# State copies moved from VectorE to ScalarE in a two-direction Mamba scan, with the chunk loops written out

## What is computed

```python
xz = x @ win.T;  u, z = split(xz)                 # 1024 channels each
u = silu(causal_conv4(u) + bconv)
dbc = u @ wx.T;  dt, B, C = dbc[:, :32], dbc[:, 32:48], dbc[:, 48:64]
delta = softplus(dt @ wdt.T + bdt);  A = -exp(Alog)
h_t = exp(delta_t * A) * h_(t-1) + (delta_t * u_t) * B_t     # 16 states n per channel
y_t = sum over n of h_t * C_t, + u * Dp, * silu(z);   y @ wout.T
```

## Time and profile before

| | |
|---|---|
| median of 3 runs | 7603.56 us (7603.14 to 7606.13) |
| profiled execution, its own time | 7600.66 us |
| its span in the profile | 7598.7 us |
| busy share of the span | PE 90%, DVE 92%, ACT 80%, POOL 92% |
| granted TensorE clock, mean | 0.973 |

### The profile page before, as it was taken

One profiled execution on the slowest core, in us unless ns is written; L12 is line 12 of the kernel. 1 busy time (PEld: TensorE's weight loads), 2 busy tenths in 40 slices (PEclk: granted clock), 3 DMA queues, 4 the chain that ended last, 5 costly groups with the idle time before them and its releaser, 6 DMA issues. The chain is left out here.

```text
span 7598.7 us, 137446 instructions
## 1 busy us (share of the span) xinstructions
PE 6830.6 (90%) x32682; PEld 4035.6 (53%) x32682; DVE 6955.4 (92%) x10093; ACT 6069.6 (80%) x11545; POOL 6968.9 (92%) x3774
## 2 busy tenths in 40 slices
PE   6899999899898989999898999999898999999889
PEld 3455555555555555555555555555555555555455
DVE  2799999999999999999999999999999999999766
ACT  1788888888788888888788888888788888888645
POOL 0899999999999999999999999999999999999678
PEclk8999999999999999999999999999999999999999
DMA  8444445444444454444445544444355444444555
GB/s 258 145 137 134 128 139 149 128 120 144 132 134 126 141 150 124 123 143 138 122 129 145 149 113 136 139 137 134 117 150 149 107 141 135 138 130 131 152 193 172
DMA packets 605609, 1066.02 MB, mean 140 GB/s; under 512 B 113584, under 2 KB 221872, under 8 KB 596336
## 3 DMA queue, kind: packets, MB, share of 16 engines
q1 hardware_dynamic: 602704, 1055.84, 46.9%
q10 hardware_dynamic: 2080, 1.05, 0.0%
HBM read 926.61 MB, written 130.05 MB: 139 GB/s over the span
## 5 line engine op out<-in xcount | busy, mean ns | idle before, releaser
L692 POOL TENSOR_TENSOR dBu<-Bb,du 128x1024 f32<-128x1024 f32 x2048 | 4787.8, 2365 | 74.9 <-DVE hV L1153 44.2
L1153 DVE TENSOR_TENSOR_SCAN scans<-scans,state,dBu 128x512 f32<-128x512 f32 x2304 | 2902.8, 1280 | 393.6 <-ACT scans L806 363.1
L806 ACT ACTIVATE scans<-delta,A 128x512 f32<-128x512 f32 x4096 | 2745.7, 691 | 557.4 <-DVE hC L1169 480.9
L1016 PE MATMUL yT<-ident,hC 128*128 128x128 f32 x9216 | 1407.4, 282 | 344.1 <-DVE hC L1169 340.8
L1169 DVE TENSOR_TENSOR hC<-scans,Cb 128x512 f32<-128x512 f32 x2304 | 1556.8, 680 | 12.2 <-PE yT L1016 12.2
L1016 PEld LDWEIGHTS yT<-ident,hC 128*128 128x128 f32 x9216 | 1058.6, 143 | 774.8 <-DVE hC L1169 536.4
L701 POOL TENSOR_TENSOR hR<-hR,Cb 128x512 f32<-128x512 f32 x1024 | 1290.0, 1270 | 190.2 <-DVE state L1183 183.7
L1153 DVE TENSOR_TENSOR_SCAN hR<-scans,state,dBu 128x512 f32<-128x512 f32 x1024 | 1293.4, 1263 | 0.5
L1009 PE MATMUL bg<-u,comb 128*128 128x512 f32 x2112 | 989.1, 594 | 0.9 <-DVE u L1125 0.9
L1153 DVE TENSOR_TENSOR_SCAN hV<-scans,state,dBu 128x512 f32<-128x512 f32 x768 | 968.6, 1261 | 13.1 <-ACT scans L806 12.8
L948 PE MATMUL bg<-hT,win_u 128*128 128x512 f32 x2112 | 966.5, 598 | 0.9 <-ACT hT L728 0.9
(11 more groups left out here) (163 smaller groups left out, 7586.9 us busy)
## 6 DMA issues: line engine op xcount, KB each, us to landing
comb<-pre_scratch SPq DMA_DIRECT2D x1040, 256.0 KB, 4.6
Bb<-bc_scratch SPq DMA_DIRECT2D x264, 512.0 KB, 8.6
Cb<-bc_scratch SPq DMA_DIRECT2D x264, 512.0 KB, 7.9
win_u<-in_win SPq DMA_DIRECT2D x264, 256.0 KB, 4.9
pre_scratch<-pre SPq DMA_DIRECT2D x264, 256.0 KB, 3.7
comb<-comb_scratch SPq DMA_DIRECT2D x66, 1024.0 KB, 8.0
win_z<-in_win SPq DMA_DIRECT2D x257, 256.0 KB, 2.7
part_scratch<-pre SPq DMA_DIRECT2D x132, 256.0 KB, 2.0
```

Source lines behind the costliest of these rows:

```text
L692: pool.tensor_tensor(dBu[:, q % AHEAD], Bb[:, 2 * q:2 * q + 2, :], du[:, j % 2, :].unsqueeze(1).broadcast_to([P, 2, T]), ALU.mult).then_in ...
L806: act.activation(place(n)[:], delta[:, j % 2, :], ACT.Exp, scale=A[:, v % 2, j * N + n:j * N + n + 1]).then_inc(dA_made, 1)
L1016: ins = nc.tensor.matmul(yT[:, tt * P:(tt + 1) * P], product[:, tt * P:(tt + 1) * P], ident[:], start=first and tt == 0, stop=False, is_tr ...
L1153: nc.vector.tensor_tensor_scan(to, place(n)[:], dBu[:, q % AHEAD, k, :], state[:, c:c + 1], ALU.mult, ALU.add).then_inc(h_made, 1)
```

## The change

Four parts.

1. VectorE's four L1183 copies a tile go. ScalarE gets four copies a tile in a new helper `keep_states`, called after each dA(n): for n = 3 and 4 after dA(8), n = 7 after dA(11), n = 1, 5, 9 after dA(13), n = 11 after dA(15). They raise the same semaphores.
2. SyncE's wait before a `Cb` load of an ASIDE pair is on `hR_used` (TensorE has added the product to `yT`) where it was on `hR_made`.
3. The four `Fori` loops become Python loops over all 32 chunks: no jump, and semaphore targets become constants. SyncE's loops stay.
4. Conditions such as `isinstance(c, int)` become `c > 0`, with the same meaning.

```diff
-TURN = 8
...
                         if 2 * q in ASIDE or 2 * q + 1 in ASIDE:
-                            sp.wait_ge(hR_made, aside(last, 2 * q + 2))
+                            sp.wait_ge(hR_used, aside(last, 2 * q + 2) + R0)
...
+            def keep_states(g, j, n):
+
+                for ns, places, saved in [(ns, hR, aside_saved) for ns in COPIES] + [(TURNED, hV, turned_saved)]:
+                    if n != ns[-1] + 4:
+                        continue
+                    act.wait_ge(h_made, g * N + ns[-1] + 1 + H0)
+                    k = (ASIDE if places is hR else TURNED).index(ns[0])
+                    step = ns[1] - ns[0] if len(ns) > 1 else 1
+                    act.copy(state[:, j * N + ns[0]:j * N + ns[-1] + 1:step],
+                             places[:, k:k + len(ns), T - 1]).then_inc(saved, 1)
...
-            with act.Fori(0, CHUNKS // TURN) as r:
-                for v in range(TURN):
-                    i, s = r * TURN + v, v % 2
...
+            for i in range(CHUNKS):
+                s = i % 2
...
-                            step_dA(g, j, v, 2 * q)
+                        step_dA(g, i, j, 2 * q)
+                        keep_states(g, j, 2 * q)
...
-                            step_dA(g, j, v, 2 * q + 1)
+                        step_dA(g, i, j, 2 * q + 1)
+                        keep_states(g, j, 2 * q + 1)
...
-                            for n in pair:
-                                for ns, places, saved in [(ns, hR, aside_saved) for ns in COPIES] + [(TURNED, hV, turned_saved)]:
-                                    if n != ns[-1]:
-                                        continue
-                                    dve.wait_ge(h_made, g * N + n + 1 + H0)
-                                    k = (ASIDE if places is hR else TURNED).index(ns[0])
-                                    step = ns[1] - ns[0] if len(ns) > 1 else 1
-                                    nc.vector.tensor_copy(state[:, j * N + ns[0]:j * N + n + 1:step],
-                                                          places[:, k:k + len(ns), T - 1]).then_inc(saved, 1)
```

More of the change, by code:

```diff
@@ L680, in _ @@
             steps(0, 0, 0, MT)
-            with pool.Fori(0, CHUNKS // TURN) as r:
-                for v in range(TURN):
-                    i, s = r * TURN + v, v % 2
[L684 to L706, removed]
@@ new lines, in _ @@
+            for i in range(CHUNKS):
+                s = i % 2
+                for j in range(MT):
+                    g = i * MT + j
+                    pool.wait_ge(du_made, g + 1)
+                    for q in range(NQ):
+                        p = j * NQ + q
+                        pool.wait_ge(h_made, g * N + 2 * (q + 1 - AHEAD) + H0)
+                        if j == 0:
+                            pool.wait_ge(B_loaded[q], i * 16 + 16)
+                        pool.tensor_tensor(dBu[:, q % AHEAD], Bb[:, 2 * q:2 * q + 2, :],
+                                           du[:, j % 2, :].unsqueeze(1).broadcast_to([P, 2, T]),
+                                           ALU.mult).then_inc(dBu_made, 1)
+                        for n in ASIDE:
+                            if q == JOINS[n]:
+                                k = ASIDE.index(n)
+                                pool.wait_ge(aside_saved, copied(g, n) + A0)
+                                if j == 0:
+                                    pool.wait_ge(C_loaded[n // 2], i * 16 + 16)
+                                pool.tensor_tensor(hR[:, k, :], hR[:, k, :], Cb[:, n, :], ALU.mult).then_inc(hR_made, 1)
+                        if q == 6:
+                            m, ms = (j + 1, s) if j + 1 < MT else (0, 1 - s)
+                            pool.wait_ge(dA_made, g * N + DU0)
+                            pool.wait_ge(dBu_made, g * NQ + 1)
+                            steps(g + 1, m, ms, i * MT + 2 * MT)
@@ L732, in take_u @@
                 act.wait_ge(bg_ready, made)
-                if m < 2 and not isinstance(c, int):
+                if m < 2 and c > 0:
                     act.wait_ge(out_stored[m], c * 32 + O0)
                 act.wait_ge(hist_stored, stored)
-                if not isinstance(c, int) or m >= 2:
+                if c > 0 or m >= 2:
                     act.wait_ge(pre_stored[m % 2], c * 64 + (m // 2) * 16)
@@ L843, in _ @@
             act.wait_ge(bg_free, PRO)
-            with act.Fori(0, CHUNKS // TURN) as r:
[L845 to L855, removed]
-                            step_dA(g, j, v, 2 * q)
[L857 to L867, removed]
-                            step_dA(g, j, v, 2 * q + 1)
[L869 to L880, removed]
-                                    continue
[L882 to L891, removed]
-                                if kind == "C":
[L893 to L912, removed]
-                                    else:
-                                        silu_z(freed(i, f"Z{m}"))
-                                nc.scalar.preload_act_table_set(EXP_LN)
@@ L944, in project_u @@
                 pe.wait_ge(wu_loaded[m % RING], (c * per + m // RING + 1) * 16)
-                if m == 0 and not isinstance(c, int):
+                if m == 0 and c > 0:
                     pe.wait_ge(bg_free, freed(c - 2, "H3"))
```

201 lines of the change are left out of this document (133 added, 68 removed).

## The result

| | before | after |
|---|---|---|
| median, 12 runs each | 7603.35 us | 7616.39 us (7609.59 to 7631.04) |
| ratio | | 1.0022, 95% interval 1.0013 to 1.0031 |
| profiled execution, its span | 7598.7 us | 7613.5 us |
| mean granted TensorE clock | 0.973 | 0.963 |

What follows compares the result with a forecast made beforehand. Bound: a chain on VectorE with holds handed on by ScalarE, TensorE full in tiles 1 and 2. Per chunk 2.05 - 0.4 - 0.5 = 1.15 us, 37 us in all, plus 30 us of jumps: 67 us off, 7535 us, range 7430 to 7600.

Steps and rivals of the forecast that it cites:

- the hold at scan 14: VectorE's scan 14 waits for GpSimd's dBu 7 after the late product of states 3 and 4: 0.5 us a chunk.
- the cover: In tile 5, time from dBu 7's end on GpSimd to scan 14's start: 2.97 us, 2.1 left after the change.
- The rival: Late copy holds VectorE at scan 14 of each tile, mean 0.6 us a tile: 7672 us, chance 0.09.
- Relief, by tiles: VectorE without its four copies a tile: 4.9 us a chunk relieved, 2.05 counted after giving each tile only its room.
- The 0.67 us counted for tile 0: Tile 0: relief of 0.24 plus 0.7 us, limited to TensorE's idle time there, 0.67 us.
- a sign against TensorE as the bound: Tiles 1 and 2: if they got shorter with TensorE still full, reading TensorE as a bound was wrong.
- The first rival: All of the relief on VectorE counts, 156 + 30 us less ScalarE's 13 us: 7428 us, chance 0.2.
- ScalarE's copies: Four small copies a tile on ScalarE, 0.1 us each taken, 0.4 us a chunk in all, 0.8 at the upper bound.
- Loops: Three loop jumps on VectorE, each a 10.3 us wait for instructions, vanish: 30 us saved.
- The third Bb load: SyncE issues it later, behind a Cb load; may reach GpSimd up to a microsecond late; counted zero, but thin.

Runs made afterwards that it cites:

- the filler: 22 transposes of the identity added on TensorE in the last pair of each chunk's last tile, against the changed kernel: 7584.53 us, ratio to before 0.9965.
- both filler kernels: The changed kernel, and the one with loops written out and all copies on VectorE, each with 22 added TensorE transposes a chunk: 0.9965 and 0.9954.
- late steps: Changed kernel with GpSimd's delta and du of the next tile made after dBu 7, not before it: 7553.21 us, ratio to before 0.9920.
- loops only: Changed kernel with all four copies back on VectorE and SyncE's old wait, loops written out: 7568.52 us, ratio to before 0.9943.
- single copies: Loops written out, hV copy on ScalarE, hR copies on VectorE with states 3 and 4 as two 128x1 copies: 7549.11 us, ratio to before 0.9912.

## Why the prediction was wrong

**The failed step: the hold at scan 14, "0.5 us a chunk, from tiles 4 and 5".** It measured 5.0 us a chunk of idle time at that scan, in all tiles but 3 and 6. The mechanism, its place and even the figure of tile 5 were right: the product 3.4 us later was forecast (9.18 us after the tile's first scan before, 12.66 after, from the earlier trace rows and the rows above, so 3.5), and 1.3 us of hold (1.34). What failed is the carry to the other tiles. I had read the cover, 2.97 us, in tile 5 alone, and let a delay "halfway", 1.9 us, fit under 2.1. Two rows of tile 1 of the kernel before would have sufficed, dBu 7 on GpSimd and scan 14:

```profile
2871.38 2.37 POOL L692 TENSOR_TENSOR dBu<-Bb,du 128x1024 f32<-128x1024 f32 x1
...
2875.50 2.46 DVE L1153 TENSOR_TENSOR_SCAN scans<-scans,state,dBu 128x512 f32<-128x512 f32 x2
```

That is 1.75 us of cover, and 1.5 us once the copies are gone. Worked out in the same way and averaged over chunks 3 to 29, the raw cover was 1.65 to 1.83 us in tiles 0 to 3 and 7, and 2.95 to 4.34 us only in tiles 4 to 6, while the product came 1.2 to 3.5 us later in the tile. I had paired a cover from one of the roomy tiles with a delay from tile 0, and that delay was off too: 0.4 us forecast, 1.7 us measured. The rows of GpSimd in tile 0, before and after:

```profile
2824.85 11.65 POOL L692 TENSOR_TENSOR dBu<-Bb,du 128x1024 f32<-128x1024 f32 x5
```

```profile
2837.80 11.62 POOL L689 TENSOR_TENSOR dBu<-Bb,du 128x1024 f32<-128x1024 f32 x5
2849.63 2.51 POOL L698 TENSOR_TENSOR hR<-hR,Cb 128x512 f32<-128x512 f32 x2 [0.22 <-ACT state L814]
```

The five dBu ahead of the product end 9.9 us into the tile before and 11.4 us after, and then GpSimd waits only 0.22 us for the copy. So GpSimd carries the delay of the tile before into this one; the step had looked at each tile by itself. ScalarE's dA(8) is later too in this tile (10.7 us in, at 2848.73, where it had been 9.5), but that goes with the half clock and is not what delays the product: with the filler dA(8) is back at 9.5 us, and the product still starts 11.3 us in. The rival gave "0.32 us a tile" as the point from which it decides; the mean hold is 0.63.

**What the step lacked altogether: TensorE's clock.** The rival priced the hold at its own length, 7672 us. In part the hold only moved idle time that VectorE had at the tile's end anyway; then it cost more where nobody had looked. The runs split the miss, as far as the filler's own price is the same in both kernels. Beside straight loops the copies were to bring 37 us, 0.49%. With the filler in both kernels they cost 0.11% (0.9965 against 0.9954), without it 0.79%. So about 0.60% of the miss is hold and relief wrongly sized, and about 0.68% goes through the clock, for which the sum had no term. The clock is at full in both filler kernels, and tile 7 shows the hold there by itself: VectorE has no idle time in it before, and it gets 0.6 us longer on average (25.6 to 26.2), a hold of 0.85 less the 0.24 of the copies. In tile 5 the hold is 1.36 us and the tile gets no longer. The last rows of the last tile on TensorE, before and after:

```profile
3038.10 0.60 PE L1016 MATMUL yT<-ident,hR 128*128 128x128 f32 x4
3040.57 1.32 PE L1016 MATMUL yT<-ident,hC 128*128 128x128 f32 x8 [1.86 <-DVE hC L1169]
```

```profile
2835.59 0.87 PE L1025 MATMUL yT<-ident,hR 128*128 128x128 f32 x4 [1.58 <-POOL hR L698]
2837.50 1.97 PE L1025 MATMUL yT<-ident,hC 128*128 128x128 f32 x8 [1.05 <-DVE hC L1176]
```

Before, the product of state 11 was ready when TensorE came to it. Now it too is late, TensorE stands 1.58 us for it and 1.05 us more after it, and the same eight products behind take 1.97 us in place of 1.32: the clock has fallen, and it is still down when the full stretch of tile 0 begins. That the half clock costs the time is shown by the filler. That it falls because of these waits is my reading: the clock at the chunk's start is 0.67 to 0.69 in the three kernels with all four copies on ScalarE and the old place of the steps, and 0.90 to 0.94 in the others without filler. The late steps keep a 1.5 us wait of TensorE for that product and still have 0.91. The clock falls there too, in 21 of 31 chunks, but it is back at full 1.3 us after the chunk's first scan (median), where it takes 4.5 us in the changed kernel. So the single wait does not make the whole loss.

**Relief, by tiles.** What could be tested held roughly. Moving the hV copy alone should bring time in tile 4 and none in tile 5; the windows of tile 4 read 27.00 us with loops only and 26.00 with the hV copy gone, those of tile 5 28.20 and 29.20. As a sum, the ratios say 0.2%, not separable from nothing. The 0.67 us counted for tile 0 did come once the clock was whole: between the two filler kernels tiles 0 to 2 together go from 80.0 to 79.3 us on average. Tile 1 is then shorter with TensorE still full, which the prediction named as a sign against TensorE as the bound; but what the three tiles lose is little more than TensorE's idle time in tile 0 (0.5 us, now nil), so the bound stands for them as one stretch. With all copies away and no hold (the late steps) 0.23% is left against loops only, 17 us, where 1.65 us a chunk, 53 us, was forecast as relief less ScalarE's cost. In that kernel VectorE's first scan waits in seven of eight tiles, 0.7 to 2.5 us each in one chunk, behind ScalarE in six of them. The first rival, 7428 us, and with it the rule of the Trainium skill, page "Perfetto Trace Analysis", section "Optimizing Scalar/DVE Operations", that a saturated VectorE may gain by moving work to ScalarE, came nowhere near: saturation was real, and the moved result had a third engine waiting for it.

**ScalarE's copies** take what was taken: 0.20 us, next start 0.08 us later.

```profile
2984.69 0.19 ACT L814 COPY state<-hR 128x2 f32<-128x2 f32 x1
2984.77 1.92 ACT L803 ACTIVATE scans<-delta,A 128x512 f32<-128x512 f32 x3
```

**Loops.** 30 us forecast, 43 us measured (33 to 53 by the interval); beside the copies on ScalarE, 1.0064 against 1.0022, 32 us. The step was right; the two profiled executions differ by 30.8 us (7598.7 and 7567.9), and why the medians differ by more stays open. The Trainium skill, page "Runtime: NRT & Kernel Launch", section "Instruction fetch mechanics", says that a jump out of the fetched window makes the engine wait for a fetch; the trace agrees, with three waits of up to 10.3 us on VectorE that straight code doesn't have.

**The third Bb load** moved, from 14.5 us ahead of the chunk's first scan to 8.5 us, and hurt nobody that the ratios show: GpSimd waits for B 4.8 us in all, 1.3 us before. Had the hold been sized from all tiles and priced at its own length, as the rival did, the sign would have come out right, but by luck: with the clock whole the same holds leave a kernel that is faster than the one before (0.9965).

## What to carry to other kernels

When a step moves to another engine, list who waits for its result and read that consumer's slack in every tile, not in one: an engine that is busy 26.1 of 26.3 us carries a delay into the next tile, and makes it up only where it has idle time, as in tiles 3 and 6 here. A copy is cheap on the engine that is in time for the next consumer; "fewest microseconds on the fullest engine" led to the slower kernel, and moving two GpSimd instructions was worth more than the four copies. And look for the stretch in which TensorE has no idle time: what TensorE does just ahead of it can decide its clock there, as the filler shows.

## What the runs showed of the hardware

- A 128x2 or 128x3 copy within SBUF on VectorE can wait for GpSimd's current instruction to end: up to 2.43 us and 1212 ns on average for 128x2 in one kernel, and every one over 0.25 us ends within 0.03 us of the end of a GpSimd instruction. A 128x1 copy within SBUF was not held in any of these profiles: the longest of the 1024 in the kernel with single copies takes 148 ns. Nor was a 128x2 copy out of PSUM (512 in the kernel before, 162 ns at most).
- Added TensorE work can shorten a kernel: 22 transposes a chunk, 43 us. It did so only in the kernel whose clock was at 0.69 there; in three others, at 0.91 to 0.92, the same filler came out 0.1% to 0.3% slower.
- A wait that the profile put down to "issue" was a wait for GpSimd that ended 0.09 us before; an equal kernel with loops had it under its right name.
